# Cross-attention and quantised feed-forward: queries turned by transfers and VectorE, probabilities in PSUM, weights cast on ScalarE

## The reference

```python
q = layernorm(x)
scores = einsum('bqd,bkd->bqk', q, ctx) / sqrt(512); scores = where(mask, -1e9, scores)
atted = einsum('bqk,bkd->bqd', softmax(scores), ctx)
x = x + einsum('bdl,ol->bdo', swapaxes(atted, -1, -2), W_merge) + b_merge
xq = quant(layernorm(x))          # one scale over the whole tensor
h = quant(silu(xq @ Wg.T) * (xq @ Wu.T))   # quant of weights: one scale per row
out = x + h @ Wd.T
```

## Time and profile before

| | |
|---|---|
| profiled execution | 548.55 us |
| its span, first to last instruction | 546.8 us |
| TensorE busy | 529.6 us (97%) |
| VectorE busy | 434.7 us (79%) |
| ScalarE busy | 298.5 us (55%) |
| GpSimd busy | 149.9 us (27%) |
| mean granted clock of TensorE | 0.989 |
| DMA | 93.60 MB, 171 GB/s |

### The profile page before, as it was taken

The page is one execution under the profiler, slowest core; times in us unless marked ns, Lnnn a source line. Parts: engine busy times, 40 slices in busy tenths (PEclk is TensorE's granted clock), DMA queues, the critical chain, the costliest instruction groups (busy, mean ns, idle before and its releaser), DMA issues. The chain is left out here.

```text
span 546.8 us, 7319 instructions
## 1 busy us (share of the span) xinstructions
PE 529.6 (97%) x2440; PEld 347.2 (64%) x2440; DVE 434.7 (79%) x805; ACT 298.5 (55%) x445; POOL 149.9 (27%) x100
## 2 busy tenths in 40 slices
PE   5979999999999999999999999999999999999996
PEld 4868888888888888888887444444444444344442
DVE  5586998969889699797668587788778778699984
ACT  3657765756557565585430635544553533976610
POOL 3657346745466454564231000000000000000000
PEclk9979999999999999999999999999999999999999
DMA  8916669495695956942376439779301101779774
GB/s 277 263 56 154 169 177 173 165 235 169 177 142 181 234 164 178 158 174 77 112 77 180 170 100 296 218 141 326 96 19 38 38 0 59 307 275 397 257 263 154
DMA packets 77599, 93.60 MB, mean 171 GB/s; under 512 B 36096, under 2 KB 54528, under 8 KB 75008
## 3 DMA queue, kind: packets, MB, share of 16 engines
q1 hardware_dynamic: 77568, 93.21, 60.9%
HBM read 59.77 MB, written 25.43 MB: 156 GB/s over the span
## 5 line engine op out<-in xcount | busy, mean ns | idle before, releaser
L1257 PE MATMUL gu<-hid,gu_T 128*128 128x512 f16 x704 | 152.3, 379 | 0.5 <-DMA hid<-hid 0.5
L1257 PEld LDWEIGHTS gu<-hid,gu_T 128*128 128x128 f16 x704 | 68.7, 98 | 84.0 <-issue 1.0
L1076 ACT ACTIVATE hid<-gu,gu_mul 128x512 f32<-128x512 f32 x88 | 59.6, 685 | 74.3 <-PE gu L1257 69.8
L1154 DVE SCALAR_TENSOR_TENSOR hid<-gu,gu_mul,hid 128x512 f32 (+1 forms) x88 | 65.0, 746 | 34.0 <-PE gu L1257 30.0
L1298 PE MATMUL gu<-wd_T,gu_T 128*128 128x512 f16 x264 | 58.0, 379 | 1.0 <-DVE gu_T L1198 0.9
L819 PE MATMUL mm<-wm_hi,p_hi 128*128 128x512 f32 x128 | 53.7, 420 | 3.2 <-DVE wm_lo L547 3.2
L1100 ACT ACTIVATE h<-hid,inv 128x512 int8<-128x512 f32 (+3 forms) x32 | 44.2, 1456 | 17.2 <-DVE gu_T L1198 13.4
L1162 DVE TENSOR_REDUCE hmax<-hid 128x1 f32 (+2 forms) x48 | 53.1, 1119 | 0.0
L819 PE MATMUL mm<-cT_hi,qT_hi 128*128 128x512 f32 x128 | 51.1, 399 | 1.9 <-DVE cT_lo L541 1.9
L821 PE MATMUL mm<-wm_hi,p_lo 128*128 128x512 f32 x128 | 51.2, 400 | 0.0
L820 PE MATMUL mm<-wm_lo,p_hi 128*128 128x512 f32 x128 | 50.9, 398 | 0.0
(11 more groups left out here) (136 smaller groups left out, 917.2 us busy)
## 6 DMA issues: line engine op xcount, KB each, us to landing
h_dram<-hid SPq DMA_DIRECT2D x3, 2816.0 KB, 9.3
hid<-h_dram SPq DMA_DIRECT2D x3, 2816.0 KB, 13.0
cb<-in_ctx_dram SPq DMA_DIRECT2D x28, 256.0 KB, 8.4
cx<-in_ctx_dram SPq DMA_DIRECT2D x7, 1024.0 KB, 11.3
x<-in_x_dram SPq DMA_DIRECT2D x5, 1024.0 KB, 5.8
x_dram<-x SPq DMA_DIRECT2D x20, 256.0 KB, 2.4
xq<-x_dram SPq DMA_DIRECT2D x5, 1024.0 KB, 12.1
x<-x_dram SPq DMA_DIRECT2D x5, 1024.0 KB, 6.2
```

What stands on the lines that cost most here:

```text
L1076: nc.scalar.activation(silu[SILU_AT[i]], gu[2 * (i % 3)][:], ACT.Silu, scale=gu_mul[:, 0, i:i + 1]).then_inc(silu_done, 1)
L1154: nc.vector.scalar_tensor_tensor(hid[:, b % SLOTS, i * L:(i + 1) * L], gu[2 * (i % 3) + 1][:], gu_mul[:, 1, i:i + 1], silu[SILU_AT[i]], AL ...
L1257: last = nc.tensor.matmul(gu[2 * (i % 3) + g][:], gu_T[:, g, h, i * P:(i + 1) * P], xT[p][:, h, :], start=h == 0, stop=h == T - 1)
```

## The change

It has six parts, all in `attention()`.

1. For batches 2 to 7 the queries are no longer transposed on TensorE. When the four `norm1` of a batch are done, 16 transfers SBUF to SBUF (64 KB each: 32 partitions by 4 by 128 values) move 32-row blocks of `qn` into a new tile `qb`: eight issued by SP (`move_q`), eight by ScalarE (`move_half`). VectorE turns 32x32 blocks in place (`turn_q`), ScalarE writes the high part (`query_hi`), GpSimd the low part (`query_lo`).
2. ScalarE issues all of `norm1(n+1)` and then its eight transfers ahead of `probs_hi(n,3)`; `row_bias1(n+1)` moves forward on VectorE, ahead of the first `turn_c`.
3. The probabilities of batches 1 to 7 are written to the PSUM banks `tr`, which the transposes no longer use; the SBUF buffers go.
4. `weights16` moves from VectorE to ScalarE, in place in `wst`.
5. GpSimd's `c_lo` comes in four pieces, and the reciprocal roots of the second normalisation of batches 0 to 6 in one operation at the end instead of seven.
6. SP's order: `load_c(n)` in batch n behind the weight transposes, the context blocks ahead of x, `d_scale` read at the start of `ffn()`. Masks: two quarters a batch earlier, two between the exponents.

```diff
+                def probs(n, t):
+                    return tr[t][:] if n else qb[:, t % 2, :]
...
+                    def move_q(n):
+                        sp.wait_ge(q_ready, T * (n + 1))
+                        if n > 2:
+                            sp.wait_ge(qT_ready, T * (n - 2))
+                        for a in range(2):
+                            for k in range(P // BLK):
+                                sp.dma_start(qb[a * BLK:(a + 1) * BLK, :, k * P:(k + 1) * P],
+                                             qn[k * BLK:(k + 1) * BLK, :, a * P:(a + 1) * P]).then_inc(q_moved, 16)
...
                         if n:
+                            sp.wait_ge(c_ready, T * n)
+                            load_c(n)
                             sp.wait_ge(w_done, through(n - 1, w_turns))
                             load_w(n)
+                            if n < B - 1:
+                                move_q(n + 1)
                             for t in range(T):
                                 store_x1(n - 1, t)
                         if n < B - 2:
+                            sp.wait_ge(cT_ready, T * (n + 1))
+                            load_cb(n + 2)
...
                             load_x(n + 2)
-                            sp.wait_ge(cT_ready, T * (n + 1))
-                            load_cb(n + 2)
-                        if n < B - 1:
-                            sp.wait_ge(c_ready, n + 1)
-                            load_c(n + 1)
...
+                        for t in range(T):
+                            nc.gpsimd.tensor_tensor(c_lo[:, t, :], cx[:, t, :], c_hi[:, t, :].bitcast(F32),
+                                                    ALU.subtract).then_inc(c_ready, 1)
...
+                    def query_lo(n):
+                        for t in range(T):
+                            gp.wait_ge(qT_hid, T * (n - 2) + t + 1)
+                            nc.gpsimd.tensor_tensor(columns(qT_lo, t), blocks(qb[:, t, :]), columns(qT_hi, t).bitcast(F32),
+                                                    ALU.subtract).then_inc(qT_ready, 1)
...
                             make_rstd1(n + 1)
                             turned_lo(n + 1)
+                            if n:
+                                query_lo(n + 1)
                         make_c_lo(n)
-                        if n:
-                            make_rstd2(n - 1)
-                    make_rstd2(B - 1)
+                    make_rstd2(0, B - 1)
+                    make_rstd2(B - 1, B)
...
+                    def move_half(n):
+                        act.wait_ge(q_ready, T * (n + 1))
+                        if n > 2:
+                            act.wait_ge(qT_ready, T * (n - 2))
+                        for a in range(2, P // BLK):
+                            for k in range(P // BLK):
+                                nc.scalar.dma_start(qb[a * BLK:(a + 1) * BLK, :, k * P:(k + 1) * P],
+                                                    qn[k * BLK:(k + 1) * BLK, :, a * P:(a + 1) * P]).then_inc(q_moved, 16)
+
+                    def query_hi(n, t):
+                        act.wait_ge(qb_turned, T * (n - 2) + t + 1)
+                        if t == 0:
+                            act.wait_ge(s_done, T * n)
+                        nc.scalar.activation(columns(qT_hi, t), blocks(qb[:, t, :]), ACT.Copy).then_inc(qT_hid, 1)
...
+                            else:
+                                if t < 2:
+                                    make_mneg(n, t + 2)
+                                if t:
+                                    probs_hi(n, t - 1)
                         if not start:
+                            if not last:
+                                for t in range(T):
+                                    norm1(n + 1, t)
+                                move_half(n + 1)
                             probs_hi(n, T - 1)
                         if not last:
-                            for k in range(T):
-                                turned_hi(n + 1, k)
-                                norm1(n + 1, k)
+                            for t in range(T):
+                                turned_hi(n + 1, t)
+                                if start:
+                                    norm1(n + 1, t)
                         context_hi(n)
+                        if not (start or last):
+                            for t in range(T):
+                                query_hi(n + 1, t)
                         for k in range(T):
+                            mixed_hi(n, k)
...
+                            if not last and k in (1, 2):
+                                make_mneg(n + 1, k - 1)
                         weights_round(n)
+                        weights16(n)
...
+                    def turn_q(n, t):
+                        if t == 0:
+                            dve.wait_ge(q_moved, 256 * (n - 1))
+                        nc.vector.transpose(qb[:, t, :], qb[:, t, :]).then_inc(qb_turned, 1)
...
-                        if not start:
-                            weights16(n - 1)
                         for t in range(T):
                             mask_and_max(n, t)
...
                                 if t == 3 and not last:
+                                    row_bias1(n + 1)
                                     for k in range(T // 2):
                                         turn_c(n + 1, k)
...
                         weights_scale(n)
+                        if not (start or last):
+                            for t in range(T):
+                                turn_q(n + 1, t)
                         for k in range(T):
...
-                                if not last:
-                                    transposed_lo(n + 1, T + k)
                                 mixed_lo(n, k)
...
                     def scores(n, k):
                         if n:
                             pe.wait_ge(g_ready, T * (n - 1) + k + 1)
+                        if n > 1:
+                            pe.wait_ge(qT_ready, T * (n - 2) + k + 1)
...
-                                if not last:
-                                    transposes(n + 1, T + k)
                                 mixed(n, k)
```

More of the change, by code:

```diff
@@ L74, in cross_attention_ffn @@
         gu_scale = keep("gu_scale", [P, 2, NI], F32)
-        d_scale = keep("d_scale", [P, D], F32)
+        scale_stored = whole.enter_context(nc.semaphore("scale_stored"))
         ln2 = keep("ln2", [P, B, 5 * T], F32)
@@ L218, in w_columns, with as8, as16 @@
                     return 2 * len(gu_tiles(n)) * D + (I if n % 2 else 0)
+                def as8(cols):
+                    return wst8[:, 4 * cols.start:3 * cols.start + cols.stop]
+                def as16(cols):
+                    return wst16[:, cols.start + cols.stop:2 * cols.stop]
                 def through(n, count):
@@ L595, in mask_and_max @@
                         dve.wait_ge(mneg_made, T * n + t + 1)
-                        if t >= 3:
-                            dve.wait_ge(p_ready, T * n + t - 2)
+                        if n == 0 and t >= 2:
+                            dve.wait_ge(p_ready, t - 1)
+                        elif n:
+                            dve.wait_ge(p_ready, T * (n - 1) + t + 1)
                         nc.vector.tensor_tensor_reduce(
-                            out=probs[t % 3][:], in0=mm[t][:], in1=mneg[:, t, :], scale=-SCALE, scalar=-LOWEST,
+                            out=probs(n, t), in0=mm[t][:], in1=mneg[:, t, :], scale=-SCALE, scalar=-LOWEST,
                             op0=ALU.add, op1=ALU.min, accum_out=nmax[:, t:t + 1]).then_inc(masked, 1)
@@ L771, in _ @@
                                 aggregate2(n - 1, k)
-                            variances2(n - 1)
-                    weights16(B - 1)
+                            if last:
+                                variances2(0, B - 1)
                     early_distances()
@@ L800, in transposes @@
                             pe.wait_ge(q_ready, T * n + g - T + 1)
-                            if n > 1:
-                                pe.wait_ge(t_lo, turns(n - 1, g))
-                            elif n == 0 and g == 2 * T - 1:
+                            if n == 0 and g == 2 * T - 1:
                                 pe.wait_ge(t_lo, turns(n, 0))
@@ L827, in scores @@
                             pe.wait_ge(g_ready, T * (n - 1) + k + 1)
-                        pe.wait_ge(t_lo, turns(n, T + k) if n else max(turns(0, T + k), turns(0, T - 1)))
+                        if n > 1:
+                            pe.wait_ge(qT_ready, T * (n - 2) + k + 1)
+                        else:
+                            pe.wait_ge(t_lo, turns(n, T + k) if n else max(turns(0, T + k), turns(0, T - 1)))
                         if n and k == 0:
@@ L931, in ffn @@
                 d_mul = sb("d_mul", [P, D], F32)
+                d_scale = sb("d_scale", [P, D], F32)
+                scale_in = sem("scale_in")
                 spare = sb("spare", [P, 1], F32)
```

89 lines of the change are left out of this document (45 added, 44 removed).

## The result

The changed kernel takes **583.81 us** (median of 6 runs, 582.81 to 585.58); the kernel before took 547.87 beside it (6 runs, 545.85 to 548.6). The ratio is 1.0668, 95% interval 1.0648 to 1.0689: slower by 36 us, where I had forecast slower by 21. The profiled execution is 583.64 us long, 35.09 more than that of before.

What follows compares the result with a forecast made beforehand. TensorE bounded the old kernel at 34.58 us a batch; the new order's rings would set 37.5. 548.55 + 18.6 (batch 7's scores) + 1.4 (late roots) + 1.3 (clock) = 569.9, predicted 569 us; range 543 to 584, the forecast's own 561 to 576.

Steps and rivals of the forecast that it cites:

- These marks: Signs of being right: two TensorE waits a batch, periods 36 to 39, ScalarE idle 3 to 4 us, VectorE waiting for `rstd1`.
- a sign of being wrong: On VectorE: `rstd1` already made when `row_bias1` comes, or no idle time on ScalarE between `norm1` and the last `probs_hi`.
- the issues cost nothing: Rival, ScalarE: issuing the eight transfers does not hold the engine; 547 us, near 548 by the skill page; chance 0.13.
- TensorE stays the bound: Rival, whole batch: other engines keep up and TensorE gains 11.5 us from the removed transposes; 538 us, chance 0.10.
- longer issues or landings: Rival, the query transfers: 0.67 us per issue gives 579 us, landings 2 us late add 12 more; chance 0.17.
- the size of `move_half` on ScalarE: Eight transfer issues ahead of the last `probs_hi`, taken at 0.46 us each, 3.7 us together, ending at r+6.8.
- the start of `norm1`: On ScalarE: first `norm1` 0.2 us after r, for a small bias operation of 0.14 us plus two handovers.
- The one taken, over ScalarE: Ring through ScalarE, from r past scores at r+23.0, rounding, `weights16` and exponents to the next `rstd1`: period 37.5 us.
- My third count, 36.3: Batch period anchored at the scores: r 13.3 us after them, the next scores 23.0 us later.
- GpSimd was put at 17.2: GpSimd's chain from r+20.1: `query_lo`, `make_c_lo`, `add_bias`, `make_rstd1`; 17.2 us (15.9 to 18.3), closing a ring of 37.3 us.
- the 4 us less that I had worked out for both low ends: GpSimd's sum with both low ends, as probabilities in PSUM end the lockout between `add_bias` and VectorE: about 4 us less.
- The clock term of batch 7: TensorE's lowered clock after the gap before scores, not hidden by other engines in batch 7: +1.3 us.

Runs made afterwards that it cites:

- e6: e1 with the context's high parts (`turned_hi`) also put ahead of ScalarE's eight issues; 541.48 us, ratio 0.9885.
- e8: e6 with query turns and roundings interleaved with the `mixed` parts, and the roots of batches 0 to 5 made a batch earlier; 538.88 us.
- e3: The changed kernel with all 16 transfers issued by SP and none by ScalarE; 557.22 us, ratio 1.0181.
- e1: The changed kernel with the last `probs_hi` moved ahead of the four `norm1` and ScalarE's eight issues; 548.29 us, ratio 1.0018.
- e4: The changed kernel with 16 unused products added on TensorE ahead of `mixed` in batches 1 to 6; 588.89 us, ratio 1.0762.
- e9: e6 with the variances and roots of batches 0 to 5 made a batch earlier; 541.09 us, ratio 0.9897.
- e11: The kernel of e9 timed again beside that of e8 on the same chip; 540.41 us, ratio 0.9869.

## Why the prediction was off, step by step

**The mechanism held in the main.** TensorE waits twice a batch, for the residual and for `g_lo`; ScalarE stands idle before the last `probs_hi`; VectorE's whole block hangs behind it. These marks came in kind, but larger than written: periods of 39.6 to 40.5 instead of 36 to 39, ScalarE idle 5.3 us instead of 3 to 4. One mark did not come, and one that I had named as a sign of being wrong did: in the batches that move queries VectorE finds `rstd1` made when `row_bias1` comes. Counting from r, the end of `rstd1`, was a mistake in the path: r has 1.2 us to spare, and `norm1` hangs on the last exponent. The transposes are really gone (e6: 32.77 a batch; forecast 32.67), and the rivals in which the issues cost nothing or TensorE stays the bound fail for this order. In another order TensorE is the bound: e6 and e8 land at 541 and 539, near the 538 worked out for that rival. The issues last as long there, but hold nothing that is needed soon. The rival that came true for this order is the one to which I had given 0.17, longer issues or landings, and of it the issues alone: the landings were no matter.

**The step that failed is the size of `move_half` on ScalarE**: "I take 0.46, the row where the queue is not full". It is 0.65, close to the upper of the two rows of SP: 5.2 us instead of 3.7 in the batch shown, 5.44 in the mean. The reason for the choice was wrong too: ScalarE's queue had nothing else in it, and the issues took as long all the same. On SP the same transfers are as dear: single issues are 0.60 us in the median when SP makes all 16 (e3), and 0.62 on SP and 0.63 on ScalarE when both issue (the changed kernel, and e1 the same). Why these take longer than the 0.46 of the context loads was not tested. The Trainium skill, "DMA: Bandwidth & Descriptors", section "Issuing engines are not separate DMA queues", has the initiation as usually small; the trace contradicts it for transfers of this size, 0.65 us against a landing of 2.3 to 2.4 in the median, and the time of 548 worked out by it belongs to no run of this order.

**The second error is the start of `norm1`.** I put it 0.2 behind r; it is 1.5, because ScalarE's order has the last exponent and the last but one `probs_hi` ahead of it, and I had counted these as done. No run takes this term out by itself; it is read from the trace.

From r = 181.50 the forecast and the trace then run in parallel. In this batch `norm1` ends at r+4.4 (forecast 3.1), issues at r+9.6 (6.8), `probs_lo` at r+11.1 (8.2), the residual at r+18.7 (15.9), scales at r+21.4 (18.7), the last `query_hi` at r+24.5 (21.9), scores at r+25.7 (23.0). Every term behind the issues is right to 0.3 us here (in the three batches that also scale a down tile they are 0.4 us longer together); the 2.7 between the ends are 1.3 of `norm1` and 1.5 of the issues.

**Which ring.** The one taken, over ScalarE, is the one that closes. In the batch from r = 181.50 to r = 220.67 (39.2 us; forecast 37.5): scores at r+25.7 (forecast 23.0), rounding 1.6 behind them (1.9), rounding and `weights16` 4.4 (4.8), first exponent to the end of `rstd` 7.4 (7.8). So 2.7 too little ahead of the scores, 1.0 too much behind them. My third count, 36.3, was the same ring added up once more, with r 13.3 behind the scores where the first had 14.5; the trace has 13.4 to 14.0, so that half of it was the better one. GpSimd was put at 17.2 and took 16.1, below the 16.2 that its low rows add up to (I wrote 15.9), and waited. The Trainium skill, "SBUF — State Buffer", section "SBUF: two separate sides", has GpSimd and a VectorE operation with two SBUF inputs lock each other out, and agrees with these pieces (`add_bias` 5.04 against 6.22 with the probabilities in PSUM), but the 4 us less that I had worked out for both low ends did not come, since that ring was not the one that closed.

In sum: batch 2's scores at 87.60 instead of 84.66 (+2.9), then five periods of 39.96 in the mean instead of 37.5 (+12.3): +33.85 where I had +18.6. These 15.2 us, by terms: the issues 6 x 1.7 = +10.4, the start of `norm1` 6 x 1.3 = +7.8, the rest ahead of the scores +1.1, the way behind the scores 5 x 0.74 = -3.7, the first r at 61.29 instead of 61.66 -0.4. The end of attention and the second part take off another 1.5. So the miss of 13.7 (583.64 - 569.9) is 19.3 us of errors the one way and 5.6 the other, and that the latter made the number nearer is luck.

**The smaller terms.** The 28-column root took 4.81 us (taken: 4.5), and with it batch 7 is 1.7 longer (taken: 1.4), mostly as TensorE's wait before the second part. The clock term of batch 7, +1.3, did not come: the half-clock stretch fell into the merge stage ahead of it and was over when the scores began. But the clock fell in every batch, at 3.2 to 6.1 us of idle time, and e4 shows that "within a ring that is hidden" was right. The transfers were hidden (forecast: by 3.5 us); they landed in 2.3 to 2.4 us in the median where I had taken 8.4 from context loads, so even SP alone nearly keeps up. Probabilities in PSUM cost nothing: in the mean `exps` takes 0.65 there and 0.72 in SBUF, `probs_lo` 0.75 and 0.88.

**The range.** 583.8 is at the very end of the range of 543 to 584 and outside the forecast's own 561 to 576. The rival with 0.67 each gives 579; the other error of the same sign, 1.3 us six times, was in none of the rivals.

## What to carry to other kernels

Issuing a DMA is work of the engine whose queue it is: here 0.60 to 0.63 us each in the median, and eight of them in front of one activation are 5.2 to 6.0 us, once per batch. Give many small transfers to an engine that has nothing else to do, or put them behind everything that another engine waits for; ask of each instruction behind them who waits for it, one after the other, because the stall moves to the next one (`p_hi`, then `cT_hi`, then nobody). When the transposes that a change removes are the bound, their 1.9 us a batch are only to be had if every other chain has that much slack: the same change was worth +36 us or -6 us by the order of a few lines.

## What was unexpected of the hardware

- An issue of 64 KB, SBUF to SBUF, held its queue's engine 0.60 us in the median (SP alone, 96 of them, e3), 0.62 and 0.63 (SP and ScalarE together, the changed kernel), single ones up to 1.4; the transfer itself landed in 2.0 us at least.
- Issues can run beside an activation that is under way (three of 0.59 to 0.62 within `turned_hi`), but the next activation does not start until the issues ahead of it are through.
- A four-column operation of VectorE between SBUF tiles took 0.17 us with GpSimd idle, 0.93 and 1.32 while a GpSimd piece ran, ending within 0.1 us of that piece's end.
- GpSimd's power over 128 partitions took 1.02 us for 4 columns, 4.15 for 24 and 4.81 for 28.
- TensorE, filled by 16 products to keep its clock, ran `mixed` at full clock, idled 2.01 us and had its clock lowered all the same 1 us into the scores. The same wait does not always end alike: before the scores of batch 2, e9 idled 2.59 us and stayed at a granted 1.00, e11 idled 2.55 and was granted 0.84 over the next 10.7 us.
